# The chosen tokens' stage with row-tiled scores, projections between the attention's units, products of halves and norms tile by tile

## What is computed

```python
scores = x @ w_router
_, idx = jax.lax.top_k(scores, CAP)                  # CAP = 256
x_sel = jnp.take_along_axis(x, idx[:, :, None], axis=1)
h = rmsnorm(x_sel, g1)
qkv = (h @ W_qkv.T).reshape(Bq, CAP, 3, H, HD)       # 16 heads of 32
att = jnp.einsum('bqhd,bkhd->bhqk', q, k) / math.sqrt(HD)
att = jax.nn.softmax(jnp.where(mask, -jnp.inf, att), axis=-1)   # causal
o = jnp.einsum('bhqk,bkhd->bqhd', att, v).reshape(Bq, CAP, Dq)
x_attn = o @ W_out.T
h2 = rmsnorm(x_sel + x_attn, g2)
x_ff = jax.nn.silu(h2 @ W1.T) * (h2 @ W2.T) @ W3.T   # hidden width 1365
out = x.at[jnp.arange(Bq)[:, None], idx].set(x_sel + x_attn + x_ff)
```

## Time and profile before

| | |
|---|---|
| median of 3 runs | 1896.87 us (1894.29 to 1896.98) |
| the profiled execution | 1893.54 us, of which the span of the trace is 1891.6 us |
| mean granted TensorE clock | 0.938 of full |
| busy in the span | PE 85%, PEld 49%, DVE 65%, ACT 46%, POOL 31% |
| chosen tokens' stage in the trace | about 535.7 us to 826.2 us, 290.5 us |

### The profile page before, as it was taken

How to read it: one execution, slowest core, us unless ns; L and a number is a source line. 1 busy time by engine, 2 the same in 40 slices (tenths; PEclk the granted TensorE clock), 3 DMA queues, 4 the chain that set the end, 5 groups by cost and what they waited for, 6 DMA issues and landing times. The chain is left out here.

```text
span 1891.6 us, 25177 instructions
## 1 busy us (share of the span) xinstructions
PE 1608.8 (85%) x9298; PEld 936.1 (49%) x9331; DVE 1237.0 (65%) x1988; ACT 870.6 (46%) x1398; POOL 587.6 (31%) x577
## 2 busy tenths in 40 slices
PE   4788888987778879947899999999998778888886
PEld 3444444443434644424566666566665544444443
DVE  3467778887431433224477777577676699999995
ACT  3355555554422623223433333333432387777773
POOL 3123333233221300012211202112121098777770
PEclk9899999999788989978899999999999999999999
DMA  4112211112630334331102012020110340122211
...
DMA packets 73158, 142.35 MB, mean 75 GB/s; under 512 B 8289, under 2 KB 17653, under 8 KB 72778
## 3 DMA queue, kind: packets, MB, share of 16 engines
...
## 5 line engine op out<-in xcount | busy, mean ns | idle before, releaser
L2549 POOL TENSOR_TENSOR E_y<-E_y,E_centre 128x1024 f32<-128x1024 f32 x64 | 151.2, 2363 | 9.7 <-ACT E_y L2578 7.8
L2464 PE MATMUL E_OP<-E_w2q,E_yb 128*128 128x512 bf16 x509 | 126.4, 405 | 25.2 <-issue 18.9
L1322 ACT ACTIVATE D_oT<-D_OB 128x512 fp32r<-128x512 f32 x64 | 38.3, 599 | 225.0 <-DVE D_OB L1663 225.0
L2541 POOL TENSOR_SCALAR E_centre<-E_hs,E_cw,E_cb 128x512 f32<-128x512 f32 x64 | 108.6, 1697 | 58.5 <-DVE E_hs L2631 58.3
L2454 PE MATMUL E_HP<-E_xT,E_w1q 128*128 128x512 bf16 x482 | 120.9, 390 | 2.1 <-DVE E_hs L2631 0.2
L1628 DVE TENSOR_TENSOR D_q_low<-D_PJ,D_q_high 128x512 fp32r<-128x512 f32 x62 | 42.9, 692 | 118.4 <-ACT D_q_high L1298 118.4
L1400 PE MATMUL D_PJ<-D_xT_high,D_wq_high 128*128 128x512 f32 x248 | 106.8, 431 | 9.2 <-DVE D_wq_low L1635 7.2
L2640 DVE SCALAR_TENSOR_TENSOR E_y<-E_hs,E_cw,E_y 128x512 f32<-128x512 f32 x128 | 106.7, 872 | 0.0
L1400 PE MATMUL D_PJ<-D_xT_high,D_wq_low 128*128 128x512 f32 x248 | 100.2, 404 | 0.0
L1400 PE MATMUL D_PJ<-D_xT_low,D_wq_high 128*128 128x512 f32 x248 | 99.6, 402 | 0.0
L2464 PEld LDWEIGHTS E_OP<-E_w2q,E_yb 128*128 128x128 bf16 x512 | 51.9, 103 | 93.6 <-issue 45.5
...
## 6 DMA issues: line engine op xcount, KB each, us to landing
...
```

Source lines behind the costliest of these rows:

```text
L2464: mm = pe.matmul(OP[:, :], yb[:, k, c * P:(c + 1) * P], w2q[:, k, :], start=k == 0, stop=k == MC - 1)
L2541: pool.tensor_scalar(U[i % 2][:, 0, :], hs[i % NBUF][:, 0, 1:TILE + 1], cw[:, 2 * p, 1:2], cb[:, 2 * p:2 * p + 1], ALU.mult, ALU.add).then ...
L2549: pool.tensor_tensor(y, y, U[i % 2][:, :, :], ALU.add).then_inc(t0, 1)
```

## The change

**All large products in three products of halves.** W_qkv, W1, W2, W3, the normalised rows and the gated rows are each split into a high half (ACT, a copy to float32r) and a low half (DVE, a subtraction; POOL for the gated rows). A product with q, k, v, W1, W2 or W3 is then three float32r products. W_out stays plain float32. Of W_qkv three parts are split during the norm, four after it, five between the units. W1 and W2 are split per column tile, two tiles ahead. W3 is split once the last product with W2 is made, since its high half shares memory with W1.

**Row-tiled scores.** Keys and queries are no longer spread with zeros: each head's product reads its own 32 rows. The products of a unit's scores go four heads at a time, and `scores_for_max` is laid out over three banks, three heads together and then the fourth, behind a wait of PE on its own work (`m_three`). DVE takes four reductions in place of two. The mask products stay of full height.

**Order.** Blocks 1 and 2 become one, and 3 and 4 one. Seven of the twelve q, k, v outputs are made ahead of the units (`HEAD`), five at the ends of the first five units. The weighing of a unit moves behind the next unit's scores, with two probability tiles. Six of the 16 measured pieces move ahead of the units. W1 and W2 are loaded after the twelfth output, behind the 16 pieces in SP's queue, as their memory is shared. **Norms** go tile by tile: square with its sum on ACT, inverse root on POOL, scaling on DVE. The second norm is woven into the product with W_out. The last products go in two pairs of row tiles.

```diff
+with ExitStack() as over:
+    gl = place(over, "gated_low", [P, MF, SEL], F32R)
+with ExitStack() as over:
+    wqkv = place(over, "wqkv", [P, KD, 3 * D])
+wl = sb("wqkv_low", [P, KD, 3 * D], F32R)
+with ExitStack() as over:
+    fl = place(over, "ffn_in_low", [P, KD, SEL], F32R)
+wout = sb("wout", [P, KD, D])
...
+with ExitStack() as over:
+    w3h = place(over, "w3_high", [P, MF, D], F32R)
+with ExitStack() as over:
+    wh = place(over, "wqkv_high", [P, KD, 3 * D], F32R)
+    hh, hl = (place(over, "hT_" + n, [P, KD, SEL], F32R) for n in ("high", "low"))
+with ExitStack() as over:
+    w12 = [place(over, f"w{i}", [P, KD, DFF]) for i in (1, 2)]
+w12l = [sb(f"w{i}_low", [P, KD, DFF], F32R) for i in (1, 2)]
+with ExitStack() as over:
+    w12h = place(over, "w12_high", [P, 2, 2, KD, P], F32R)
...
+def turn_rows(pe, n, normed, turned):
+    pe.wait_ge(normed, n + 1)
     for k in range(KD):
...
+        mm = pe.transpose(PS[:, k, n * P:(n + 1) * P], hn[:, n, k * P:(k + 1) * P], cst["ident"][:, :])
...
+units = [(b, j) for j in range(QT) for b in range(NB)]
+UN = len(units)
+q, k_, v = 0, QT, 2 * QT
+outs = [q, k_, q + 1, v, v + 1, v + 2, v + 3, k_ + 1, q + 2, k_ + 2, q + 3, k_ + 3]
+HEAD = 7
+bank_of = [4, 5, 6, 7, 0, 1, 2, 6, 7, 6, 7, 6]
+V_AT = outs.index(v)
+whole, tile_cols = slice(0, KD), lambda m: slice(m * P, (m + 1) * P)
+parts = [(whole, tile_cols(m)) for m in outs[:V_AT]] + [(slice(k, k + 1), slice(2 * D, 3 * D)) for k in range(KD)]
+parts += [(whole, tile_cols(m)) for m in outs[HEAD:]]
+parts_for = lambda i: i + 1 if i < V_AT else max(i + 1, V_AT + KD)
+lows_until = lambda i: sum(m < v for m in outs[:i])
+AHEAD = 3
+new_parts = [range(AHEAD, V_AT + KD)] + [()] * (HEAD - 2) + [range(i, i + 1) for i in range(HEAD, len(parts))] + [()]
+EARLY = 6
+piece_at = lambda n: range(EARLY + 2 * n, min(EARLY + 2 * n + 2, WP))
...
+        sp.wait_ge(made, len(outs))
+        for w, n in zip(w12, ("W1T", "W2T")):
+            sp.dma_start(w[:, :, :], io[n].rearrange("(k p) n -> p k n", p=P)).then_inc(later_in, 16)
...
+            pe.wait_ge(w_lo, parts_for(i))
+            for k in range(KD):
+                if i == 0:
+                    pe.wait_ge(h_lo, k + 1)
+                for t, (w, h) in enumerate(((wh[:, k, cols], hh), (wl[:, k, cols], hh), (wh[:, k, cols], hl))):
+                    x = h[:, k, :] if c < 0 else h[:, k, c * P:(c + 1) * P]
+                    w, x = (w, x) if c < 0 else (x, w)
+                    mm = pe.matmul(bank, w, x, start=(k, t) == (0, 0), stop=(k, t) == (KD - 1, 2))
+            mm.then_inc(made, 1)
...
+            for g in range(LAST):
+                ask(g, g, slice(0, P), first, first, True)
+            for g in range(LAST):
+                hide(g, slice(0, P))
+            for g in range(LAST):
+                ask(g, g, slice(P, W), second, both, True)
+            for g in range(LAST):
+                mm = hide(g, slice(CAP, W))
+            mm.then_inc(m_three, 1)
+            pe.wait_ge(m_three, n + 1)
+            for bank, (asked, known) in enumerate(((first, first), (second, first), (second, second))):
+                ask(LAST, bank, slice(W, W + P), asked, known, bank != 1)
+                if bank != 1:
+                    mm = hide(bank, slice(W, W + P))
...
-            if n + 1 < len(units):
-                scores_for_max(n + 1)
+            for cols, h, asked in ((slice(0, CAP), first, both), (slice(CAP, W), second, second)):
+                for kp, qp, start in ((qkh, qkh, True), (qkl, qkh, False), (qkh, qkl, False)):
+                    for g in range(HG):
+                        pe.matmul(PS[:, g, cols], keys(kp, g, j, b, h),
+                                  qp[rows(g), j, b * CAP + asked.start:b * CAP + asked.stop], start=start, stop=False)
+                for g in range(HG):
+                    pe.matmul(PS[:, g, cols], cst["pick"][rows(g), g, :], mT[rows(g), asked], start=False, stop=False)
+                for g in range(HG):
+                    mm = pe.matmul(PS[:, g, cols.start:cols.start + P], identb[:, :], lo, start=False, stop=True)
+                    if h is second:
+                        mm.then_inc(s_mm, 1)
...
+        pe.wait_ge(w_in, 16 * 4)
+        for n in range(NS):
+            turn_rows(pe, n, out, turned)
+        for i in range(HEAD):
+            project(i)
+        pe.wait_ge(ev, V_AT + 1)
+        pe.wait_ge(low, V_AT)
+        pe.wait_ge(mask_ok, 1)
+        scores_for_max(0)
+        turn_maxima(0)
+        pe.wait_ge(ev, HEAD)
+        for n in range(UN):
+            scores(n)
+            if n + 1 < UN:
+                i = min(HEAD + n, len(outs))
+                pe.wait_ge(low, lows_until(i))
+                scores_for_max(n + 1)
+            if n:
+                weigh(n - 1)
+            if n + 1 < UN:
+                turn_maxima(n + 1)
+            if HEAD + n < len(outs):
+                project(HEAD + n)
+        weigh(UN - 1)
...
+        act.wait_ge(w_in, 16 * 4)
+        for n in range(NS):
+            act.activation(hn[:, n, :], xs[:, n, :], ACT.Square, accum_out=ss[:, n:n + 1]).then_inc(stat, 1)
+            if n < AHEAD:
+                high_w(n)
+        act.wait_ge(turned, NS)
+        for k in range(KD):
+            act.activation(hh[:, k, :], PS[:, k, :], ACT.Copy).then_inc(h_hi, 1)
+        for i in range(HEAD):
+            for part in new_parts[i]:
...
+        keep_mT(0)
+        for n in range(UN):
...
+            for i in piece_at(n)[0:1]:
                 measure_piece(act, wb, i)
...
+            if n + 1 < UN:
+                keep_mT(n + 1)
+            if HEAD + n < len(outs):
+                keep(HEAD + n)
+            for i in piece_at(n)[1:]:
+                measure_piece(act, wb, i)
...
+            banks = PS[:, MB:MB + LAST, :]
+            dve.tensor_reduce(mx[:, 0, 0:LAST], banks[:, :, 0:P], AX.X, ALU.max).then_inc(m_mx, 1)
+            dve.tensor_reduce(mx[:, 1, 0:LAST], banks[:, :, P:W], AX.X, ALU.max).then_inc(m_mx, 1)
+            dve.tensor_reduce(mx[:, 0, LAST:HG], banks[:, 0, W:W + P], AX.X, ALU.max).then_inc(m_mx, 1)
+            dve.tensor_reduce(mx[:, 1, LAST:HG], banks[:, 1:LAST, W:W + P], AX.XY, ALU.max).then_inc(m_mx, 1)
...
+        for n in range(NS):
+            mean_square(dve, n, stat, ve)
+            if n < AHEAD:
+                low_w(n)
+            if n:
+                normalise(dve, n - 1, 0, sc, out)
+        normalise(dve, NS - 1, 0, sc, out)
+        dve.tensor_copy(mask[:, :, :], maskf[:, :, :]).then_inc(mask_ok, 1)
+        for k in range(KD):
+            dve.wait_ge(h_hi, k + 1)
+            dve.tensor_tensor(hl[:, k, :], PS[:, k, :], hh[:, k, :].bitcast(F32), ALU.subtract).then_inc(h_lo, 1)
...
+        for n in range(UN):
+            if n + 1 < UN:
+                maxima(n + 1)
+            if HEAD + n < len(outs):
+                for part in new_parts[HEAD + n]:
+                    low_w(part)
+            if n:
+                divide(n - 1)
+            if HEAD + n < len(outs):
+                low_qk(HEAD + n)
+        divide(UN - 1)
...
+        for i in range(2):
+            load_piece(sp, io, wb, i)
...
+        def project_out(n):
+            for k in range(QT):
+                mm = pe.matmul(PS[:, 4 + n, :], oT[:, k, n * P:(n + 1) * P], wout[:, k, :], start=k == 0, stop=k == QT - 1)
+            mm.then_inc(made, 1)
...
+            project_out(n)
+            if n >= 2:
+                turn_rows(pe, n - 2, out, turned)
+        for n in (NS - 2, NS - 1):
+            turn_rows(pe, n, out, turned)
+        pe.wait_ge(f_lo, KD)
+        for m in range(MF):
+            w = width(m)
+            if m >= 2:
+                pe.wait_ge(gated, m - 1)
+            for i, done in enumerate((made1, made2)):
+                pe.wait_ge(w_lo, 2 * m + i + 1)
+                high, low = w12h[:, m % 2, i, :, 0:w], w12l[i][:, :, m * P:m * P + w]
+                for k in range(KD):
+                    for t, (wt, x) in enumerate(((high, fh), (low, fh), (high, fl))):
+                        mm = pe.matmul(PS[0:w, 2 * i + m % 2, :], wt[:, k, :], x[:, k, :],
+                                       start=(k, t) == (0, 0), stop=(k, t) == (KD - 1, 2))
+                mm.then_inc(done, 1)
+        pe.wait_ge(based, NS)
+        for pair in range(NS // 2):
+            for m in range(MF):
+                w = width(m)
+                pe.wait_ge(w3_lo, m + 1)
+                pe.wait_ge(g_lo, m + 1)
+                for n in (2 * pair, 2 * pair + 1):
+                    toks = slice(n * P, (n + 1) * P)
+                    for t, (g, wt) in enumerate(((gh, w3h), (gh, w3l), (gl, w3h))):
+                        mm = pe.matmul(PS[:, 4 + n, :], g[0:w, m, toks], wt[0:w, m, :],
+                                       start=(m, t) == (0, 0), stop=(m, t) == (MF - 1, 2))
+                    if m == MF - 1:
+                        mm.then_inc(made3, 1)
...
+            for i, (wt, done) in enumerate(zip(w12, (made1, made2))):
```

(40 more changed lines are left out.)

394 lines of the change are left out of this document (161 added, 233 removed).

## The result

The changed kernel takes **1850.14 us** (median of four runs, 1847.24 to 1852.87) against 1896.92 for the kernel before on the same chip (three runs as above and one at 3971.62 us, an outlier that the ratio leaves out): a ratio of 0.9758, with a 95% interval of 0.9737 to 0.9779. In a second set of runs it came to 0.9766 (0.9753 to 0.9779). The forecast was 1848, with a range of 1832 to 1870. The profiled execution took 1849.65 us with a span of 1848.0, against 1893.54 and 1891.6 before: 43.9 us less, where my sum for the profiled execution said 48.8.

The account below looks back on a forecast made before the run. PE was taken to bound the stage except in the attention units and the W_out and norm stretch. Terms -15.9, +0.4, -2.3, -27.2 and -3.8 sum to -48.8 us: 1844.7 for the profiled execution, 1848 against the median, range 1832 to 1870.

Parts of the forecast that it names:

- (e): Rival in the units: no clock is lost and groups run at 0.12 us, giving 1830 us; 8 in 100.
- Products of halves: Feed-forward with W1, W2 and W3: three products of halves at 0.233 us each, 98.8 us against 114.7, -15.9.
- First norm: From the stage's start to the first product: 8.9 us against 11.2 before, -2.3.
- Units: Attention units: 9.75 us with a projection, 7.3 without; first product to end of units 103.3 us, -27.2.
- rival (c): A unit keeps its length and projections come on top: 12.0 and 9.1 us, giving 1863; 14 in 100.
- Rival (b): Row tiles and waits leave half clock through all the units, +37 us, giving 1885; 10 in 100.
- The last unit: End of the units: scores, exponentials, weighing and division stand bare, 8.0 us.
- Changes of mode: Switching PE's tiling mode in the units: 0.1 us each, some 14 a unit, 112 in all.
- rival (a): Changes of mode drain the array: whole gain lost at 0.54 us each, 1904 at 0.6; 3 in 100.
- Groups of four products: Row-tiled scores in a unit: 0.15 us per group of four, eight groups, scores 2.0 us against 4.23.
- W1 and W2 later: Loads after the twelfth output take 15 us, hidden ahead of the product with W_out with 7 us to spare.
- Rival (d): Halves or W1 and W2 come late, PE waiting 10 to 20 us before W_out or in feed-forward: 1862; 8 in 100.

## Why the prediction was right, point by point

The forecast of 1848 against 1850.14, and 1844.7 against 1849.65 for the profiled execution: the sum was 5 us too good. The own sum came true; of the rivals only a half of (e) did, the groups at 0.12. The agreement is better than the sum deserved, in two ways. In the stage it was 6.6 us too good (248.3 us against 290.5 - 48.8 = 241.7); 1.4 us of this came back outside the stage, where nothing was changed, such as a second attention of 666.1 us instead of 667.4. And the execution profiled before lay 3.3 us below its median, the one after only 0.5, which brings the medians to within 2 us. Both are luck. The 6.6 are 3.2 from the first product to the end of the units, 1.8 in the feed-forward, 0.8 in the first norm, 0.5 in the second and 0.3 in the tail.

- **Products of halves.** Right in mechanism and price: 63.5 us from 677.6 to 741.1 with W1 and W2, forecast 63.5; the wait ahead of W3 3.5, forecast 3.0; W3 33.6, forecast 32.3. 14.1 us gained from the start of W1 to the end of W3, forecast 15.9. The term that was mis-sized is the half clock at the start of W3, 1.5 in the sum: 5.7 us at the lower level cost 2.5. In other traces it was nothing behind the same wait, so my bounds of nothing and 3 were right and the value between them is a chance. The run with plain products gave the gain back. For the products of q, k and v no run did.
- **First norm.** 9.7 us, forecast 8.9 (before 11.2). In five traces with nothing changed ahead of the first product it took 9.2, with the lower clock ending sooner, so 0.5 us of the miss is clock. The other 0.3 stays open, and no run took the new order of the norms back.
- **Seven outputs ahead.** 20.6 us, forecast 22.6: I had put 3 us for the clock and 1.4 was lost; in five traces none was, at 19.2 us.
- **Bare maxima.** 5.8, forecast 5.3.
- **Units.** With a projection 9.67 and 9.69 at the full clock, forecast 9.75; without 7.56 (at 0.78) and 7.48 (at 0.99), forecast 7.3. So rival (c) is out. The clock over the units cost 4.8 in the first and 0.5 in each of two more, against the 4 in the sum. Rival (b) is out for this kernel: the units with a projection behind the first ran at 1.00 or 0.83, as their stretches of dense work had let me argue. How near it was shows in the run with all outputs ahead, where three of the four windows shown lie at 0.50.
- **The last unit** is the step that failed. I counted scores, exponentials, weighing and division, 8.0 us, and gave the weighing no wait. It took 10.9, because the weighing must wait for the division of the unit before, out of the same bank. Without that wait it takes 8.4.
- **Changes of mode.** 0.10 us each, as put, and rival (a) is out. But the run with 96 more took 23 us more in the units, of which only 14 are the changes and the lost side by side running. That changes could have a price also through the clock was not in the rival.
- **Groups of four products.** I took 0.15 between bounds of 0.12 and 0.23. It is the lower bound, 0.12 for 256 columns and hardly less for 128; a unit's scores take 1.89 us against 2.0.
- **W1 and W2 later.** Landed at about 641.7, some 11 us ahead of the product with W_out at 652.9, at 419 GB/s over the seventh unit. Hidden, with more to spare than forecast. Rival (d) is out.
- **Second norm.** 25.2 us, forecast 24.7.
- **Tail.** 6.3 us, forecast 6.0.

In the stage the gain was 42.2 us, and the whole span fell by 43.6.

What stays open: which mix of short products and waits brings the clock down within the units. The fillers show that giving PE work in its waits prevents most of it; but with them one unit still had 0.84 (11.0 us), and the run with fillers in two places had four units at 0.83 where the traces of the changed kernel had two and three. Nor is it settled why the same wait ahead of W3 is followed by half clock in some traces and not in others. Of the parts of the change, three have a run of their own: the halves in the feed-forward, the products side by side and the projections between the units. The halves of q, k and v and the new order of the norms have only the forecast's agreement with the trace.
